# Four GNN layers on one core: the first column of the running maximum moved to ScalarE, the steps of two attention layers reordered, and the logit layer's indices kept on chip

## The reference

```python
def gatv2_layer(x, src, dst, edge_attr, Wl, Wr, We, att, bias, concat):
    z = leaky_relu(xl[src] + xr[dst] + ee, 0.2)
    score = einsum('ehc,hc->eh', z, att)
    m = segment_max(score, dst)
    a = exp(score - m[dst])
    denom = segment_sum(a, dst)
    msg = xl[src] * (a / denom[dst])
    return segment_sum(msg, dst)

h = relu(layernorm(x)); x = x + L0(h)   # two gatv2 layers (8 heads, then 2 heads), then a small MLP
h = relu(layernorm(x)); x = x + L1(h)   # attention with scalar logits h[src]@a_src + h[dst]@a_dst
h = relu(layernorm(x)); x = x + L2(h)   # relational layer
h = relu(layernorm(x)); x = x + L3(h)   # gatv2 (4 heads), batch norm over the nodes, gelu
```

## Time and profile before

| | |
|---|---|
| median of 3 runs | 7174.21 us (7170.84 to 7176.18) |
| the profiled execution | 7206.94 us, span 7205.2 us |
| busy share of the span | POOL 66%, DVE 75%, PE 54%, ACT 44% |
| layer a | 657 to 1770 us |
| layer b | 1770 to 2877 us |
| logit block | 3453 to 4015 us |
| layer g | 5480 to 6570 us |

### The profile page before, as it was taken

How to read it: one execution, slowest core, us unless ns; L and a number is a source line. 1 busy time by engine, 2 the same in 40 slices (tenths; PEclk the granted TensorE clock), 3 DMA queues, 4 the chain that set the end, 5 groups by cost and what they waited for, 6 DMA issues and landing times. The chain is left out here.

```text
span 7205.2 us, 84156 instructions
## 1 busy us (share of the span) xinstructions
PE 3879.4 (54%) x13024; PEld 2314.5 (32%) x13024; DVE 5386.3 (75%) x16939; ACT 3173.0 (44%) x7568; POOL 4760.7 (66%) x4609
## 2 busy tenths in 40 slices
PE   0001667664666665899000689868886766772000
PEld 0000233332333333788000345763332433441000
DVE  4502888886777777888676899767887888887886
ACT  0001666664333333777444100224554666665555
POOL 1777777775777776776677556016664777774776
PEclk9999776776788887555555789558997676665555
DMA  6001555555433343111799100569994555554554
GB/s 191 4 1 29 97 99 97 99 96 79 90 85 84 85 85 72 47 47 45 112 120 115 25 7 8 158 144 131 154 153 101 115 114 115 115 114 114 165 169 137
DMA packets 915728, 687.80 MB, mean 95 GB/s; under 512 B 604705, under 2 KB 754495, under 8 KB 914973
## 3 DMA queue, kind: packets, MB, share of 16 engines
q1 hardware_dynamic: 517456, 403.54, 21.1%
q0 software_dynamic: 147200, 139.08, 19.9%
q10 hardware_dynamic: 250888, 143.42, 6.6%
HBM read 491.36 MB, written 227.64 MB: 100 GB/s over the span
## 5 line engine op out<-in xcount | busy, mean ns | idle before, releaser
L802 POOL DMA_INDIRECT b_xg<-t_H,c_at x784 | 833.2, 1063 | 284.0 <-issue 238.4
L802 POOL DMA_INDIRECT g_xg<-t_D,c_at x784 | 803.4, 1025 | 320.1 <-issue 238.2
L802 POOL DMA_INDIRECT a_xg<-t_XL,c_at x784 | 830.6, 1059 | 250.3 <-issue 238.8
L1822 POOL DMA_INDIRECT f_dg<-t_D,c_at x392 | 377.0, 962 | 555.9 <-POOLq L179 358.7
L2210 POOL DMA_INDIRECT out<-n_yo,c_at x392 | 430.9, 1099 | 235.1 <-issue 116.1
L440 POOL DMA_INDIRECT t_XL<-su_pos,su_scatx x392 | 389.8, 994 | 245.6 <-DMA t_XL<-in_nodes 126.4
L1326 POOL DMA_INDIRECT l_d<-t_D,l_ix x392 | 397.7, 1014 | 183.8 <-issue 121.4
L1141 POOL DMA_INDIRECT t_RANK<-m_place,m_at x392 | 397.9, 1015 | 163.2 <-issue 116.4
L938 ACT ACTIVATE a_hn<-a_xg,a_sm 128x64 f32<-128x64 f32 x784 | 269.8, 430 | 401.0 <-DVE a_sm L675 400.1
L1375 ACT ACTIVATE l_hn<-l_xs,l_sm 128x64 f32<-128x64 f32 x784 | 265.0, 426 | 295.6 <-DVE l_sm L675 211.9
L2189 ACT ACTIVATE n_h<-n_x,n_sm 128x64 f32<-128x64 f32 (+1 forms) x800 | 269.4, 426 | 210.0 <-DVE n_sm L675 210.0
(11 more groups left out here) (455 smaller groups left out, 14037.6 us busy)
## 6 DMA issues: line engine op xcount, KB each, us to landing
a_ends<-t_LAST SPq DMA_DIRECT2D x98, 256.0 KB, 5.1
t_XSD<-a_xg SPq DMA_DIRECT2D x98, 256.0 KB
t_H<-a_oE ACTq DMA_DIRECT2D x98, 256.0 KB
b_ends<-t_LAST SPq DMA_DIRECT2D x98, 256.0 KB
l_xb<-t_XSD SPq DMA_DIRECT2D x49, 512.0 KB
f_rl<-t_REL SPq DMA_DIRECT2D x49, 512.0 KB
g_xb<-t_XSD SPq DMA_DIRECT2D x98, 256.0 KB
g_ends<-t_LAST SPq DMA_DIRECT2D x98, 256.0 KB, 5.2
```

Of the source, the lines that this page charges most:

```text
L802: nc.gpsimd.indirect_dma_start(xg[k][:, j, i, :], None, table, bass.IndirectOffsetOnAxis(ap=C["at"][:, i, n * J + j:n * J + j + 1], axis=0 ...
L1822: nc.gpsimd.indirect_dma_start(dg[k][:, u, j, :], None, T["D2"], bass.IndirectOffsetOnAxis(ap=C["at"][:, 0, (2 * n + u) * J + j:(2 * n + u ...
```

## The change

Seven edits. (1) `maximum` no longer copies the last column of the older tile into column 0: the scan takes its start value from the older tile itself, and ACT makes the copy (`carried`, semaphore `rc`), which only `ed` needs. (2) In layer a DVE starts its step with `denominator`, and the quotients come behind the sums. (3) In layer a PE's `results` has lag 5 and stands between `project` and `scores`, and ACT's `normed` stands between `values` and `features`. (4) In layer g DVE's `norm` moves from the end of the step to its head, PE and ACT get other orders and lags. (5) Layer b gets `carried` as its first ACT stage and is otherwise as it was. (6) A tile `C["source"]` is filled by one transfer at the end of SP's part of `mlp_block`, and the logit gathers take their row numbers from it. (7) The logit gathers are written out without a loop, and SP's 49 loads of `l_ix` and its wait for the gathers are gone.

```diff
-            ch3, ch4 = Chain(dve, S["ch3"], 2), Chain(dve, S["ch4"], 1)
+            ch3, ch4 = Chain(dve, S["ch3"], 1), Chain(dve, S["ch4"], 1)
...
-                ch3(v.tensor_copy(r[k][:, 0:1], r[(k - 1) % SL][:, CH:CH + 1]))
-                ch3(v.tensor_tensor_scan(r[k][:, 1:CH + 1], bS[:, :], ends[k][:, :], r[k][:, 0:1], ALU.max, ALU.add))
+                ch3(v.tensor_tensor_scan(r[k][:, 1:CH + 1], bS[:, :], ends[k][:, :], r[(k - 1) % SL][:, CH:CH + 1],
+                                         ALU.max, ALU.add))
+                dve.wait_ge(S["rc"], n + 1)
                 v.tensor_tensor(ed[k][:, :], bS[:, :], r[k][:, 0:CH], ALU.subtract).then_inc(S["ed"], 1)
...
+            elif tag == "a":
+                stages = [(4, denominator), (3, leaky), (4, sums), (5, quotients), (3, maximum), (1, norm)]
             else:
-                stages = [(L, leaky), (L + 2, quotients), (L + 1, sums), (L, maximum), (L - 2, norm)]
-                if not both:
-                    stages.insert(2, (L + 1, denominator))
+                stages = [(1, norm), (3, leaky), (5, quotients), (4, sums), (3, maximum)]
             flow(dve, stages, slots=SL)
...
+            def carried(n, k, q, old):
+                if later(n):
+                    act.wait_ge(S["ch3"], n)
+                else:
+                    act.wait_ge(S["clear"], 1)
+                if old:
+                    act.wait_ge(S["ed"], n - SL + 1)
+                f(r[k][:, 0:1], r[(k - 1) % SL][:, CH:CH + 1], ACT.Copy).then_inc(S["rc"], 1)
...
             if wide:
-                stages = [(L - 1, features), (L - 2, turned), (L, exponents), (L + 2, results)]
+                stages = [(L, carried), (L - 1, features), (L - 2, turned), (L, exponents), (L + 2, results)]
+            elif tag == "a":
+                stages = [(3, carried), (3, values), (2, normed), (3, features), (2, turned), (3, exponents), (5, results)]
             else:
-                stages = [(L, values), (L, features), (L - 1, normed), (L - 1, turned), (L, exponents), (L + 2, results)]
+                stages = [(3, carried), (3, values), (3, features), (2, turned), (1, normed), (3, exponents), (6, results)]
...
+            elif tag == "a":
+                stages = [(3, project), (5, results), (3, scores), (2, turn)]
             else:
-                stages = [(L, project), (L, scores), (L - 1, turn), (L + 1, results)]
-            if tag == "g":
-                stages.append((L + 3, moments))
+                stages = [(2, turn), (7, moments), (3, scores), (2, project), (4, results)]
...
+            sp.dma_start(C["source"][:, :].rearrange("p (n j) -> p n j", j=LOGIT_ROWS),
+                         T["PSRC"].rearrange("(n p j) -> p n j", p=P, j=LOGIT_ROWS)).then_inc(s_source, 16)
+            sp.wait_ge(s_source, 16)
...
                 if old:
-                    sp.wait_ge(s_g[k], NG * q)
-                sp.dma_start(ix[k][:, :], words_by(T["PSRC"], n, K)).then_inc(s_ix[k], 16)
-                if old:
-                    sp.wait_ge(s_xs, n - SL + 1)
+                    hold(sp, s_spturn, (s_xs, n - SL + 1))
...
-                hold(pool, s_turn, (s_ix[k], 16 * (q + 1)))
                 if old:
                     hold(pool, s_turn, (s_xs, n - SL + 1))
...
-                        bass.IndirectOffsetOnAxis(ap=ix[k][:, j:j + 1], axis=0)).then_inc(s_g[k], 16)
-            flow(pool, [(0, gather)], total=NB, slots=SL)
+                        bass.IndirectOffsetOnAxis(ap=C["source"][:, n * K + j:n * K + j + 1], axis=0)).then_inc(s_g[k], 16)
+            flow(pool, [(0, gather)], total=NB, slots=SL, looped=False)
```

More of the change, by code:

```diff
@@ L734, in gat_block @@
         s_ps = m.sem("ps")
-        names = "gap sq bs bc ln hn hT h z zs zt xl s ed ex den rec sum o div oE turn pturn spturn clear chz ch1 ch3 ch4 tail at"
+        names = "gap sq bs bc ln hn hT h z zs zt xl s ed ex den rec sum o div oE turn pturn spturn clear rc chz ch1 ch3 ch4 tail at"
         S = {n: m.sem(n) for n in names.split()}
@@ L1121, in mlp_block @@
         s_at, s_rank, s_rturn, s_spturn = m.sems("at", SL), m.sems("rank", SL), m.sem("rturn"), m.sem("spturn")
+        s_source = m.sem("source")
         rank = T["RANK"].unsqueeze(1)
@@ L1278, in _ @@
                 act.wait_ge(s_st[k], 16 * chunks_of(k, SL))
+LOGIT_ROWS = 8
 def logit_block(nc, T, C):
@@ L1288, in logit_block @@
         SL = 4
-        K = 8
+        K = LOGIT_ROWS
         NB = EP // (P * K)
         slots = range(SL)
-        ix = [m.sb(f"ix{k}", [P, K], I32) for k in slots]
         d1 = [m.sb(f"d1{k}", [P, 2, K, D]) for k in slots]
@@ L1300, in logit_block @@
         sm = m.sb("sm", [P, 6, 2 * K])
-        s_ix, s_g, s_ld, s_hs, s_es = (m.sems(x, SL) for x in "ix g ld hs es".split())
-        s_xs, s_f, s_hn, s_e, s_ch, s_che, s_turn = (m.sem(x) for x in "xs f hn e ch che turn".split())
+        s_g, s_ld, s_hs, s_es = (m.sems(x, SL) for x in "g ld hs es".split())
+        s_xs, s_f, s_hn, s_e, s_ch, s_che, s_turn, s_spturn = (m.sem(x) for x in "xs f hn e ch che turn spturn".split())
         block = ctx.enter_context(nc.Block())
@@ L2267, in program @@
         C["at"] = m.sb("at", [P, 2, EF], I32)
+        C["source"] = m.sb("source", [P, EF], I32)
         prologue_block(nc, a, T, C)
```

## The result

Three runs of the changed kernel took 7069.28 us (7061.21 to 7070.02) against 7174.21: 105 us less. The ratio on record for the runs is 0.9842 with a 95% interval from 0.9829 to 0.9856; the two medians alone give 0.9854. The time lies 0.7 us under the range and 27 us under the forecast. Its profiled execution took 7069.28 us, so the two profiles differ by 138 us and the runs by 105.

| stage | before | after | difference | forecast |
|---|---|---|---|---|
| a, first to last gather | 1069.3 | 994.7 | -74.6 | -74 |
| b, the same | 1072.8 | 1067.1 | -5.7 | 0 |
| last rank gather to first logit gather | 51.5 | 48.7 | -2.8 | in the -4 |
| logit, first gather to the next block's first | 575.3 | 556.2 | -19.1 | -4 |
| g, first to last gather | 1042.2 | 999.6 | -42.6 | -8 |

The account below looks back on a forecast made before the run. POOL's gathers were taken to bound layers a and g, PE's transposes layer b, transfers the logit block. Terms -74 (a), 0 (b), 0 (g), -4 (logit) make -78: 7174.2 to 7096 us; range 7070 to 7160, chance 0.8.

Parts of the forecast that it names:

- Layer a: Chunks go from 10.91 to 10.1 us, DVE's mean step, with no waits for landings: 74 us less.
- The certain loss at a_num's scan: In layer a the numerator's scan holds a gather for 0.65 us every chunk; the new order removes this.
- the branch step: Layer a, one DVE step in four: the loop's branch makes `norm` to `leaky` 3.81 instead of 3.35, 0.4 us more.
- Rival 1: Layer a keeps waiting for landings at 10.7 us a chunk: only 25 to 42 us less, middle 7141; chance 0.25.
- rival 3: Layer a goes at PE's pace because scores come late: 11.4 us a chunk, 49 us more, 7219; chance 0.07.
- Rival 4: Scans starting during a gather wait for its end: layer a's DVE step 11.5 us, 58 more, 7228; chance 0.02.
- Layer g: Gather loss 0.55 us a chunk against 0.63, 8 us less, offset by a longer drain: sum 0.
- 5 (a), 11 (logit) and 30 (g): Margins in the forecast's own range, 7070 to 7125: layer a 5 either way, logit 0 to -15, g -30 to +30.
- the bound for g alone: Limits on layer g's change in gather loss: 62 us less to 30 us more.
- The drain of g: After layer g's last gather, `norm` at the head adds a whole further step: 8.4 us more.
- The logit block: Transfers set the pace, so dropping the 49 small loads gives only 4 us less; bounds 0 and 15.
- Layer b: The copy's 0.17 us off DVE changes nothing, as waits for PE's transposes set the pace: 0, bounds -10 and +5.

Follow-up runs that it names:

- a_only: The kernel before with only layer a's part of the change (orders of DVE, ACT and PE, copied column on ACT): ratio 0.9889, 7130 us.
- a_pair_kept: The changed kernel, but in layer a `leaky` is first again and the denominator's scan directly ahead of a_msg and a_num: ratio 0.9926 to before, 7129 us.
- a_copy_back: The changed kernel, but in layer a DVE makes the one-column copy again instead of ACT: ratio 0.9859 to before, 7082 us.
- g_only: The kernel before with only layer g's part of the change (`norm` at the head, PE and ACT orders and lags, copy on ACT): ratio 0.9974, 7186 us.
- logit_only: The kernel before with only the logit block's edits and the on-chip load of row numbers: ratio 0.9983, 7191 us.
- b_apart: The changed kernel, but in layer b the addition making b_oE is done between b_den and b_msg: ratio 0.9904 to before, 7110 us.

## Why the prediction was wrong where it was, and right where it was

**Layer a, right.** Forecast 74 less, measured 74.6 between the two profiles and 71 to 74 between a_only and the others of its set. The certain loss at a_num's scan is gone (63 us in a_pair_kept), and DVE's step sets the pace (a_copy_back). The mean step came out at 10.11 us against 10.1; that it fits so well is partly luck. The 3.81 that I took for the branch step holds a wait of 0.33 for ACT, so the row didn't show the branch; it costs 0.6 (10.6 against 10.0), and the other steps are 0.05 shorter than summed. Rival 1 is out, since DVE waits for a landing in 10 of 98 chunks, and a layer that waits for landings wouldn't have felt 0.17 us; so is rival 3: the maximum's scan waited for PE 2.7 us in all of the 98 chunks together. Rival 4 has nothing in its favour: a_zt and a_msg start and run beside the stretched gather of 1384.52.

**Layer g, the step that failed:** "I take half and half with a few misses, 0.55 a chunk against 0.63 now: 98 x 0.08 = 8 us less". Measured 0.31 and 0.39 with the old logit block, 0.18 and 0.19 with the new one: the layer's own edits gave 31 to 37 us (g_only's 1011 against 1042, 1045 and 1049), and the logit edits 12 to 20 more. I had the right removal, that the wait of `leaky` goes, and took it as worth nothing. But that wait, up to 1.6 us in a step, was what scattered the scan's start over 7.4 to 9.1 us after the last gather, and at 8.2 and later, where 62 of 97 chunks lay, a chunk loses 0.5 to 0.7. Without it a step from g_xg's addition to g_num's scan takes 5.93 to 6.46 us in nine chunks of ten, and the start is landing plus that; 7.74 to 8.03 is free. That the wait did the scattering is read from these distributions; no run takes the wait away alone. Measured by whole runs, g_only's 19 us and logit_only's 12 stand against forecasts of 0 and 4; these 27 us are the size of the whole miss. I also took every long gather for one beside a scan, where in layer g 36 of them belong to g_ex. I had seen two phases in the earlier trace rows and made a coin toss of them, where the sum 1.6 + 5.95 or 1.9 + 6.0 could have been laid against the gathers' grid of 1.25 us: 0.30 + 6 x 1.25 = 7.8 us for the seventh gather's start.

**The range.** Its lower end, 7070, was too high by the prediction's own terms: 7096 less 5 (a), 11 (logit) and 30 (g) is 7050, and the bound for g alone had been 62 less.

**The drain of g, right in kind:** 8.4 forecast, 6.7 between the two profiles, and 4 to 6 within a set (90.8 against 85.3 to 86.9, 91.0 against 85.1) to the next block's first gather.

**The logit block: size open, effect missed.** 4 less forecast; 6 less measured in one set and 6 more in another. That the block's end or its new tile would move the landings of layer g by 0.2 us I had no row for. Whether it is the tile's place or something that the block leaves behind stays open.

**Layer b, right:** 0 forecast, bounds -10 and +5; b_xg's stretch is 1068 to 1073 us in the table's five traces with DVE's copy and 1064 to 1070 in the eight with ACT's, b_apart left out.

**The rule behind it, sharpened.** A scan with both inputs in SBUF that has begun 0.10 us before a gather starts holds it to the scan's end and 0.76 us more; one that begins 0.04 before leaves it alone. In the twelve traces of the table with an ordinary pace of layer g, all 94 gathers that started 0.10 to 0.12 us after such a scan were held, and none of the 71 at 0.03 to 0.08. The multiplication of `sums` is stricter: it held all 87 gathers that started 0.05 to 0.08 us after it, each to its end and 0.82 us more. The Trainium skill ("SBUF — State Buffer", section "SBUF: two separate sides") says that whoever starts first blocks the other for a whole instruction. The hold of the gather agrees with it. The other half doesn't: the scan that starts 0.04 us ahead is in progress when the gather starts and both take about their usual time, 1.30 (1.28 alone) and 0.95, and DVE's operations start beside a gather that is under way.

## What to carry to other kernels

When a series of operations on a fixed grid (here a gather every 1.25 us) can be held by another engine's operation, work out where in the grid that operation starts, from the wait that resets the step, chunk by chunk; 0.06 us decided over 0.98. Take spacing from start-to-start times at the same neighbours, since a small operation costs 0.31 or 0.57 us by what follows it. And a short wait that is "hidden" still moves everything behind it. Don't subtract two profiles of different sets of runs where transfers set the pace.

## What was not expected of the hardware

- Sets of runs differ: the kernel before took 7174 to 7206 us in four of them and 8804 and 8683 in two. Kernels near the changed one, with DVE busy for 5317 to 5324 us (5326 to 5340 in their like of the other sets), were 0.5 to 0.9% slower there than before, so the gain of 1.6% may not be had everywhere. The changed kernel itself was not run there. Whether it is the chip or the time, and what holds the engines (106.7 us ahead of one small operation), is open.
- Gathers of layer g land 1.59 to 1.71 us after the last one ends with the old logit block and 1.80 to 1.88 with the new one, though that block ends 1.5 ms ahead of the layer; those of layers a and b don't move (1.52 to 1.54, where DVE waits for them, and 1.60 to 1.63).
- A one-column copy between two larger operations on DVE shifts the next by 0.06 us, ahead of a scan by 0.17.
